# One fused block, gated cross-attention and ternary feed-forward: the quantised feed-forward input turned by transposing transfers, and new instruction orders

## The reference

```python
x = x + tanh(g_xattn) * attention(layernorm(x), ctx, ctx, mask)      # 16 heads of 32, 77 keys
x = x + tanh(g_ffn) * ffn(layernorm(x))

# ffn: quantised activations, ternary weights
def _act_quant(x):
    scale = 127.0 / clip(max(abs(x), axis=-1), 1e-05)
    return clip(round(x * scale), -128, 127) / scale
gate = silu(_act_quant(z) @ ternary(w_gate).T)
up   = _act_quant(z) @ ternary(w_up).T
out  = _act_quant(gate * up) @ ternary(w_down).T
```

## Time and profile before

| | |
|---|---|
| median of 3 runs | 1466.08 us (1465.9 to 1468.2) |
| the profiled execution's own time | 1465.82 us |
| its span | 1464.0 us |
| mean granted TensorE clock | 0.972 of full speed |
| busy PE / DVE / ACT / POOL | 92% / 77% / 67% / 50% |
| mean DMA | 95 GB/s |

### The profile page before, as it was taken

The page is one execution under the profiler, slowest core; times in us unless marked ns, Lnnn a source line. Parts: engine busy times, 40 slices in busy tenths (PEclk is TensorE's granted clock), DMA queues, the critical chain, the costliest instruction groups (busy, mean ns, idle before and its releaser), DMA issues.

```text
span 1464.0 us, 28946 instructions
## 1 busy us (share of the span) xinstructions
PE 1346.3 (92%) x8576; PEld 682.9 (47%) x8896; DVE 1132.3 (77%) x2577; ACT 978.2 (67%) x1468; POOL 727.2 (50%) x1187
## 2 busy tenths in 40 slices
...
PEclk9766999999999999999999999999999999999999
...
GB/s 279 251 183 98 87 56 133 39 132 60 110 95 64 130 54 133 36 107 85 79 124 53 140 39 138 45 100 95 73 131 54 133 37 120 68 75 87 34 26 30
DMA packets 224105, 139.47 MB, mean 95 GB/s; under 512 B 161582, under 2 KB 195246, under 8 KB 222536
## 3 DMA queue, kind: packets, MB, share of 16 engines
...
...
## 4 chain that ended last, share of the span: by engine, by line
issue 27%; PE 22%; ACT 22%; DVE 14%; POOL 11%; ACTq 1%; DMA 1%; POOLq 1%; DVEq 0%; SPq 0%
PE bank L1161 13%; ACT work L669 5%; ACT work L668 4%; ACT up L707 3%; POOL region L575 3%; POOL rs L534 3%; ACT region L699 3%; DVE st L885 3%; PE bank L1183 2%; ACT region L719 2%; ACT region L711 2%; DVE fs L962 1%; DVE nmax L913 1%; DVE region L956 1%; ACT ah L678 1%
## 5 line engine op out<-in xcount | busy, mean ns | idle before, releaser
L575 POOL TENSOR_TENSOR region<-region,up 128x512 f32<-128x512 f32 x256 | 333.3, 1305 | 256.8 <-DVE region L972 169.6
L1161 PE MATMUL bank<-tern_gate,region 128*128 128x512 fp8e4 x1024 | 263.7, 380 | 8.0 <-DVE region L972 5.7
L1161 PE MATMUL bank<-tern_up,region 128*128 128x512 fp8e4 x1024 | 262.8, 379 | 0.0
L566 POOL TENSOR_TENSOR work<-work 124x512 f16<-124x512 f32 x160 | 192.7, 1212 | 101.1 <-ACT work L669 94.0
L1183 PE MATMUL bank<-tern_down,region 128*128 128x512 fp8e4 x1024 | 231.8, 379 | 11.4 <-ACT region L719 11.4
L699 ACT ACTIVATE region<-bank,fs 128x512 f32<-128x512 f32 x256 | 177.2, 698 | 75.7 <-PE bank L1161 74.8
L972 DVE SCALAR_TENSOR_TENSOR region<-region,bank 128x512 f32<-128x512 f32 x256 | 172.7, 680 | 18.7 <-ACT region L699 16.0
L707 ACT ACTIVATE up<-bank 128x512 f32<-128x512 f32 x256 | 155.3, 608 | 36.0 <-PE bank L1161 35.5
L978 DVE TENSOR_REDUCE hmx<-region 128x1 f32<-128x512 f32 x256 | 168.1, 675 | 9.9 <-POOL region L575 9.8
L711 ACT ACTIVATE region<-region,fs 128x2048 f32<-128x2048 f32 x64 | 129.0, 2015 | 58.9 <-DVE fs L989 58.9
L683 ACT ACTIVATE region<-region,fs 128x512 f32<-128x512 f32 x64 | 46.2, 722 | 181.9 <-DVE fs L965 181.9
...
## 6 DMA issues: line engine op xcount, KB each, us to landing
...
```

The source lines that it names most:

```text
L566: nc.gpsimd.tensor_tensor(p_lo[0:CR, at, :], p32[0:CR, at % PSLOTS, :], p_hi[0:CR, at, :], ALU.subtract).then_inc(p_lo_ready, 1)
L575: nc.gpsimd.tensor_tensor(ht, ht, up[:, n % 2, :], ALU.mult).then_inc(hmul_ready, 1)
L1161: ins = T.matmul(pb[2 * (n % 2) + w][:, :], xqT[:, k, tok], tern[w][:, k * FF + n * GT:k * FF + (n + 1) * GT], start=(k == 0), stop=(k == ...
```

## The change

The quantised z is turned as the attention's parts are, by a transposing transfer that SyncE issues. For that ScalarE gets a step `zb` that subtracts MAGIC and writes the whole numbers as bf16 into a new pair of buffers zb; SyncE gets a step `tz` that waits for it and, from group 1 on, for the last read of that part of xqT. `xq` goes from TensorE's and ScalarE's lists. `gu` waits for the transfer, and z's buffer is free again when zb is written.

```diff
+        zb = sb("zb", [P, 2, DM], bf16)
...
+            def z_transposed(g, t, _):
+                sp.wait_ge(zb_ready, g * TT + (t + 1))
+                if g:
+                    sp.wait_ge(up_mm, (g - 1) * (TT * FN) + (t + 1) * FN)
+                sp.dma_start_transpose(xqT[:, :, t * P:(t + 1) * P], zb[:, t % 2, :]).then_inc(xq_in[t], 16)
...
-            def xq(f, t, _):
-
-                act.wait_ge(xqT_mm, f * TT + (t + 1))
-                nc.scalar.activation(xqT[:, :, t * P:(t + 1) * P],
-                                     pb[3 - t % 2][:, 0:DM // 2].bitcast(i16).rearrange("p (c n) -> p c n", c=KC),
-                                     ACT.Copy).then_inc(xqT_ready, 1)
+            def z_integers(g, t, _):
+                act.wait_ge(z_ready, g * TT + (t + 1))
+                if t >= 2:
+                    act.wait_ge(xq_in[t - 2], g * 16 + 16)
+                elif not first(g):
+                    act.wait_ge(xq_in[t + 2], g * 16)
+                nc.scalar.activation(zb[:, t % 2, :], z[:, t % 2, :], ACT.Copy, bias=-MAGIC).then_inc(zb_ready, 1)
...
                 if t >= 2:
-                    dve.wait_ge(xqT_mm, g * TT + (t - 1))
+                    dve.wait_ge(zb_ready, g * TT + (t - 1))
...
-            def xq(f, t, _):
-
-                pe.wait_ge(z_ready, f * TT + (t + 1))
-                if t == 2:
-                    pe.wait_ge(up_ready, f * (TT * FN) + FN)
-                elif t == 3:
-                    pe.wait_ge(silu_ready, f * (TT * FN) + FN)
-                elif t == 1:
-                    pe.wait_ge(out_ready, f * TT + 1)
-                for cc in range(KC):
-                    ins = T.transpose(pb[3 - t % 2][:, cc * P // 2:(cc + 1) * P // 2].bitcast(bf16), low_words(z[:, t % 2, cc * P:(cc + 1) * P]), ident16[:, :])
-                ins.then_inc(xqT_mm, 1)
-
             def gu(f, t, n):
...
                 if n == 0:
-                    pe.wait_ge(xqT_ready, f * TT + (t + 1))
+                    pe.wait_ge(xq_in[t], f * 16 + 16)
...
-                if n == 1 and t <= 1:
-                    pe.wait_ge(xqT_ready, f * TT + 2 * t + 2)
```

All fifteen lists are written anew. Of TensorE's list for the loop the first line was and is:

```diff
-    F:xq00 F:xq10 A:q00 A:q10 A:q20 A:q30 A:s00 F:gu00 A:s01 A:s10 F:gu01 A:s11 F:gu02 A:s20 A:s21 F:gu03 A:s30
+    F:gu00 A:q00 F:gu01 A:q10 A:q20 F:gu02 F:gu03 A:s00 A:q30 F:gu10 A:s01 A:s10 F:gu11 A:s11 A:s20 F:gu12 A:s21
```

More of the change, by code:

```diff
@@ L62 @@
 TENSOR_ORDER = """
-    F:xq00 F:xq10 A:q00 A:q10 A:q20 A:q30 A:s00 F:gu00 A:s01 A:s10 F:gu01 A:s11 F:gu02 A:s20 A:s21 F:gu03 A:s30
-    A:s31 F:xq20 F:xq30 F:gu10 F:gu11 A:mT00 F:gu12 F:gu13 F:hT00 A:sc00 A:sc01 A:sc02 F:down00 A:sc03 A:sc04
-    F:gu20 A:sc10 A:sc11 F:gu21 A:pv00 F:gu22 F:gu23 A:pv01 A:sc12 F:hT10 A:sc13 A:sc14 A:pv02 F:down10 A:pv03
-    F:gu30 A:pv10 F:gu31 A:pv11 F:gu32 A:pv12 F:gu33 A:pv13 A:wo00 F:hT20 A:wo10 F:down20 F:hT30 A:wo20 F:down30
-    A:wo30
+    F:gu00 A:q00 F:gu01 A:q10 A:q20 F:gu02 F:gu03 A:s00 A:q30 F:gu10 A:s01 A:s10 F:gu11 A:s11 A:s20 F:gu12 A:s21
@@ L68 @@
+    A:s30 F:gu13 F:hT00 A:s31 A:mT00 F:down00 F:gu20 A:sc00 A:sc01 A:sc02 F:gu21 A:sc03 F:gu22 A:sc04 A:sc10
+    A:sc11 F:gu23 F:hT10 A:pv00 A:sc12 A:pv01 F:down10 A:pv02 A:sc13 A:sc14 A:pv03 F:gu30 F:gu31 A:pv10 F:gu32
+    A:pv11 F:gu33 A:pv12 F:hT20 A:wo00 A:pv13 F:down20 A:wo10 F:hT30 A:wo20 F:down30 A:wo30
 """
 SCALAR_ORDER = """
-    A:q00 A:q10 A:q20 F:xq00 F:xq10 A:q30 F:gu00 F:up00 F:gu01 F:up01 F:up02 F:gu02 F:gu03 F:up03 F:xq20 F:xq30
-    F:gu10 F:up10 F:gu11 F:up11 A:mT00 F:gu12 F:hq00 F:up12 F:gu13 F:hT00 F:up13 A:sc00 A:sc01 N:xh00 A:sc02
@@ L79 @@
-    N:xl00 F:hm12 F:hm13 F:hs10 F:gu20 A:pv00 F:gu21 F:hm20 N:xn20 F:gu22 A:pv01 A:al00 F:gu23 F:hm21 A:al01
-    F:hm22 A:pv02 F:down10 A:al02 A:pv03 F:gu30 A:pv10 A:al03 F:hm23 F:hs20 A:al10 A:pv11 F:gu31 A:pv12 A:al11
-    F:gu32 A:al12 N:xl10 F:gu33 F:hm30 F:hm31 F:hm32 A:pv13 N:xn30 F:hm33 A:wo00 F:hs30 A:wo10 A:st00 F:down20
-    A:al13 A:st10 N:xl20 N:xl30 A:zn00 A:zn10 A:za00 A:wo20 A:za10 F:down30 A:st20 A:wo30 A:st30 A:zn20 A:za20
+    N:ln00 A:q00 F:gu00 A:q10 F:gu01 F:hm00 A:q20 F:gu02 F:hm01 F:gu03 A:s00 F:hm02 F:hm03 F:hs00 A:q30 F:gu10
@@ new lines @@
+    A:s01 A:s10 F:gu11 A:s11 A:s20 F:gu12 A:s21 A:s30 F:gu13 F:hm10 A:s31 A:mh00 F:hm11 F:hm12 F:hm13 F:hs10
+    F:down00 F:gu20 F:hm20 F:gu21 N:xn00 F:gu22 A:pv00 F:gu23 N:xn10 F:hm21 F:hm22 A:al00 A:pv01 A:al01 A:pv02
+    F:down10 F:hm23 N:xl00 A:pv03 A:al02 F:hs20 A:al03 F:gu30 A:pv10 F:gu31 A:al10 A:pv11 F:hm30 F:gu32 F:hm31
+    N:xn20 F:gu33 A:al11 N:xl10 A:pv12 F:hm32 A:wo00 A:st00 A:al12 F:hm33 F:hs30 N:xn30 A:zn00 F:down20 A:za00
+    A:wo10 N:xl20 A:pv13 A:al13 A:st10 A:wo20 N:xl30 A:zn10 A:st20 F:down30 A:za10 A:wo30 A:zn20 A:st30 A:za20
@@ L131 @@
-    F:gu20 F:gu21 F:gu22 A:pv00 A:sc10 F:gu23 A:pv01 F:hT10 A:sc11 A:pv02 A:sc12 A:sc13 A:pv03 F:down10 A:sc14
-    F:gu30 F:gu31 A:pv10 F:gu32 A:pv11 F:gu33 A:pv12 F:hT20 A:wo00 A:pv13 A:wo10 F:down20 F:hT30 A:wo20 G:xq00
-    F:down30 A:wo30 G:xq10 G:gu00 G:gu01 G:gu02 G:gu03 G:xq20 G:xq30 G:gu10 G:gu11 G:gu12 G:gu13 G:hT00 G:down00
-    G:gu20 G:gu21 G:gu22 G:gu23 G:hT10 G:down10 G:gu30 G:gu31 G:gu32 G:gu33 G:hT20 G:down20 G:hT30 G:down30
+    A:q00 A:q10 F:gu00 A:q20 F:gu01 A:s00 A:q30 F:gu02 A:s01 A:s10 F:gu03 A:s11 F:gu10 F:gu11 A:s20 A:s21 F:gu12
@@ new lines @@
+    A:s30 F:gu13 A:s31 F:hT00 A:mT00 F:down00 F:gu20 A:sc00 A:sc01 A:sc02 F:gu21 A:sc03 A:sc04 F:gu22 A:sc10
+    A:sc11 F:gu23 A:pv00 F:hT10 A:pv01 A:sc12 A:sc13 A:pv02 F:down10 A:sc14 A:pv03 F:gu30 F:gu31 A:pv10 F:gu32
+    A:pv11 F:gu33 A:pv12 A:wo00 F:hT20 A:pv13 A:wo10 F:down20 F:hT30 A:wo20 F:down30 G:gu00 G:gu01 G:gu02 G:gu03
+    G:gu10 G:gu11 G:gu12 G:gu13 G:hT00 A:wo30 G:down00 G:gu20 G:gu21 G:gu22 G:gu23 G:hT10 G:down10 G:gu30 G:gu31
+    G:gu32 G:gu33 G:hT20 G:down20 G:hT30 G:down30
```

119 lines of the change are left out of this document (59 added, 60 removed).

## The result

| | before | changed kernel |
|---|---|---|
| median of the runs | 1466.85 us (6 runs, 1464.57 to 1469.40) | 1471.55 us (6 runs, 1468.89 to 1473.69) |
| ratio | 1 | 1.0031, 95% interval 1.0016 to 1.0046 |
| profiled execution, span | 1464.0 us | 1471.9 us |
| mean granted clock | 0.972 | 0.968 |

What follows compares the result with a forecast made beforehand. TensorE, busy 92% of the span, was taken as the bound. Loop -20, behind it -10.4, before it -4 make -34.4 from 1465.8: about 1431, stated as 1430 us, range 1408 to 1455.

Steps and rivals of the forecast that it cites:

- inner turns, 13: Loop turns: 78.8 us of work plus 3.1 of stalls make 81.9, which is 1.45 less a turn.
- Behind the loop: After the last loop turn: -6.5 up to the last wo, -3.9 after it, together -10.4 us, between -5 and -13.
- TensorE's work: In each turn TensorE loses 16 transposes, 0.89 us, so its work falls from 79.7 to 78.8.
- zb: ScalarE's new copy, taken at 640 ns: +0.04 a tile, 0.2 us a turn, at most 0.5.
- tz00: First z transfer of a turn: issued at -2.7, lands at -0.3, so gu00 is just in time; 0.4 us a turn charged.
- The rule against it: Skill advises TensorE for transposes; by its figures a tile takes 5.2 us by DMA instead of 2.3, making the loop longer.
- The order: Walk of TensorE's new loop list for late inputs: stalls of 3.1 us a turn against 3.7 before.
- the waits at s, at pv three times and at the last hT mostly go: In the loop, these TensorE waits mostly vanish while the one at down00 grows; stalls fall from 3.7 to 3.1 us.
- The largest stall that I named: In each loop turn, TensorE waits some 1.6 us at hT00 to down00, where 0.5 were left before.
- Before the loop: Start of the kernel: -4 us, between -12 and +4, with a 12.17 wait for query rows addressed by SyncE's new list.
- (d): Rival: z's transfer lands 4.6 us later every turn, gu00 waits 4.3 more, turns of 86.2, 1492 us; chance 0.10.
- (b): Rival: stalls only change places, 3.7 us a turn as before; loop gives -12.5, end -6, 1447 us; chance 0.20.

Runs made afterwards that it cites:

- kernel 3: Changed kernel with kv00 moved behind m00 on SyncE and pv12 moved ahead of al11 and xl10 on VectorE; 1446.83 us, ratio 0.9867.
- kernel 9: As kernel 3, but with the first turn's lists of the kernel before and q00 in front of gu00 on TensorE; 1442.87 us, ratio 0.9840.
- kernel 4: The change's transposing transfers, copies and waits with the lists of the kernel before, xq struck, zb and tz put in; 1480.90 us, ratio 1.0100.
- Run 1: Changed kernel with the next batch's key load kv00 moved behind m00 in SyncE's loop list; 1457.32 us, ratio 0.9930.
- run 12: Kernel before the change, with only kv00 moved in front of qs10 and m00 on SyncE; 1467.40 us, ratio 1.0008.
- Run 2: Changed kernel with pv12 moved ahead of al11 and xl10 in VectorE's loop list; 1460.55 us, ratio 0.9957.
- run 11: As kernel 3, but with the transfer tz00 behind the load x00 instead of in front of it on SyncE; 1570.02 us, ratio 1.0709.

## Why the prediction was wrong

The forecast's terms beside the spans (the forecast cut the first stretch at gu00, so its -20 for 14 turns stands here as 13 turns of -1.45, and the fourteenth falls to the first row):

| term | forecast | changed kernel | kernel 3 | kernel 9 |
|---|---|---|---|---|
| before the loop, with its first turn | -5.5 | +2.3 | +1.7 | -0.4 |
| inner turns, 13 | -18.9 | +15.8 | -9.8 | -9.1 |
| last attention part | -6.5 | -6.2 | -7.0 | -7.0 |
| tail | -3.9 | -4.0 | -4.2 | -4.1 |

(Of the same working for kernels 3 and 9: first and last mT at 179.17 and 1335.64, 177.05 and 1334.25; spans 1444.6 and 1443.3.)

- **Behind the loop** the prediction was right, mechanism and size: z's buffer is freed by zb, the 3.79 went, wo30 fills the wait before a down; -10.2 against -10.4.
- **TensorE's work** was right: 16 transposes less at 0.056 are 0.9, and all other matmuls of a turn are the same in number. **zb** was taken at 640 ns; the whole trace has a median of 629. **tz00** was placed just in time and is so: after the loop's first turn no wait for it is printed in the changed kernel, and one of 0.2 in ten turns of kernel 3.

```profile
L699 ACT ACTIVATE zb<-region x64: 612/629/641, 144.2 to 1440.8; 128x512 bf16<-128x512 f32 x64
L474 SPq DMA_TRANSPOSE region<-zb x64: 1188/1204/2014, 144.8 to 1441.5; - x64
...
DMA to landing us min/median/max: 2.3/2.4/6.1
```

- **The rule against it.** A tile's four blocks land 2.4 us after issue (median of 64). The Trainium skill ("VectorE: DVE Perf Modes", "The three transpose paths") has 1309 ns for one 128x128 by DMA; an estimated 5.2 us for four, taken one after another, is not what this trace shows. The Trainium skill's advice there, TensorE where it will do ("Rules for kernel authors"), is borne out all the same by kernel 4, though for another reason: the saved 0.9 us of TensorE's work a turn came back as waits, and 1.45 more.
- **The step that failed is "The order": "Walking TensorE's new list by the same durations and asking at each word who is late".** It did this once, for a regular turn, and multiplied by 14. SyncE's list was walked only from the turn's end to tz00. In three turns of the 14 kv00 is not empty, and I had not asked what stands behind it, nor what it waits for. Run 1 prices this at 14.2 us (16.3 between the profiled inner turns, some 4.6 of it by the clock in two turns of the three). Run 1 and run 12 together show that neither kv00's place nor the new order does it alone; that it is s31's place within the new order is read from the traces.
- **In the same step: "the waits at s, at pv three times and at the last hT mostly go".** Most did, but 1.42 (by the starts, 1.26 as printed) came before pv13. I walked VectorE's list at the mean durations of its lines. Those means hold two kinds of instruction, the free ones and those that begin while a product of GpSimd is running, and the new list put two of the slow kind, 2.0 us longer together, ahead of a bank that TensorE needed. Run 2 gives 11.0 us for their place; that the place alone, at the short durations, would have made no wait is worked out, not run. The largest stall that I named was right in place and size (1.6 between hT00 and down00; 1.49 measured).
- **Before the loop** the -4 had the wrong sign. I had seen that the first query would be later, and it is, by 7.1. TensorE still comes to the first wo 2.0 earlier (124.03 beside 125.98), but what decides is z: its first tile is scaled at 144.15 beside 143.87.

```profile
143.43 0.72 ACT L690 ACTIVATE region<-region,fs 128x512 f32<-128x512 f32 x1 [2.76 <-DVE fs L973]
```

  Then come the copy and a transfer that is the first of three in a row: gu00 starts 3.6 us after its issue, where I had 2.3. I had not followed the next group's last transpose in SYNC_FIRST (141.31; with the old lists both last ones go out from 131.16 or 133.18), nor weighed that gu00 as the first word leaves TensorE nothing to do while z is on its way. Run 9 takes 2.1 us of it back at the first mT.
- **The rivals.** None of them had this mechanism. (d), the slower one, put the danger on tz00's landing, which was not it; run 11 shows that the danger is real there, and that my 4.3 for a landing 4.6 later would be too little, since 2.4 us by the clock's fall came on top of 7.1 of wait. (b), stalls as large as before and 1447, is what kernel 3 does (1446.8), with 3.8 of stalls a turn.

With all that was found put back (kernel 9), 1430 is still too low by 13. By the terms of the table 9.8 are in the inner turns, most of which take 82.5 to 82.6 where I had 81.9 (3.7 to 3.8 of stalls instead of 3.1), three of them 83.1 to 83.2. Another 5.1 are at the start, and 0.7 came back behind the loop. Of the 0.7 a turn, 0.45 can be the wait that came up before the last hidden transposes in run 2; the rest was not followed.
